# Four-layer gated cross-attention model: the last feed-forward stage is cut into two staggered halves

## Reference

```python
x_norm = x * rsqrt(mean(x*x) + eps)            # x here is the layernormed input
H_res_logits = (x_norm @ W_res.T) + H_res_base # 4 x 4 a token
H_pre_logits, H_post_logits = ...              # 4 each
H_res = sinkhorn_log(H_res_logits)             # 50 iterations, tau 0.1
H_pre, H_post = softmax(H_pre_logits), softmax(H_post_logits)
g = sigmoid(gate)
H_res = (1 - g) * I + g * H_res
x_pre = einsum('btnc,btn->btc', x_streams, H_pre)
y = x_pre @ W_branch
x_mixed = einsum('btij,btjc->btic', H_res, x_streams)
out = x_mixed + einsum('btc,btn->btnc', y, H_post)
x = x + tanh(g_ffn[3]) * out
```

## Time and profile before

| | us |
|---|---|
| median of 3 executions | 1494.13 (1493.41 to 1495.05) |
| the profiled execution, its own time | 1496.6 |
| its span in the trace | 1494.5 |
| TensorE's mean granted clock, share of full speed | 0.954 |

### The profile page before, as it was taken

How to read it: one execution, slowest core, us unless ns; L and a number is a source line. 1 busy time by engine, 2 the same in 40 slices (tenths; PEclk the granted TensorE clock), 3 DMA queues, 4 the chain that set the end, 5 groups by cost and what they waited for, 6 DMA issues and landing times.

```text
span 1494.5 us, 18659 instructions
## 1 busy us (share of the span) xinstructions
PE 1345.3 (90%) x6492; PEld 966.4 (65%) x6492; DVE 1115.3 (75%) x2045; ACT 676.3 (45%) x1405; POOL 336.9 (23%) x386
## 2 busy tenths in 40 slices
PE   7999999999998999968999998999999999999104
PEld 5665566566576558747888865777777777777102
DVE  4788898898888997986555575656666666577998
ACT  4777777787523443432222224443434434343104
POOL 1112112111264020243111031221312221212620
PEclk9999999999999999999999998999999999999557
DMA  5677988798810011243211210101101201000001
GB/s 220 169 180 178 238 219 187 170 244 205 210 69 1 1 57 35 50 94 79 72 56 51 102 43 6 66 29 43 71 29 43 71 29 43 0 1 1 0 0 57
DMA packets 37910, 127.74 MB, mean 85 GB/s; under 512 B 4944, under 2 KB 10960, under 8 KB 31680
## 3 DMA queue, kind: packets, MB, share of 16 engines
q1 hardware_dynamic: 26304, 83.38, 15.9%
q0 software_dynamic: 11520, 43.26, 15.3%
HBM read 72.63 MB, written 10.75 MB: 56 GB/s over the span
## 4 chain that ended last, share of the span: by engine, by line
PE 56%; DVE 23%; DVEq 6%; ACT 5%; DMA 5%; issue 4%; POOL 1%; POOLq 0%; SPq 0%
PE PS L150 12%; PE PS L152 11%; PE PS L151 11%; DVE AR L676 4%; PE PS L925 4%; PE PS L963 4%; DMA AR<-AR 2%; ACT s_sb L606 2%; DVE AR L2654 2%; PE PS L949 2%; DMA nf_in<-in_nf 2%; DVE AR L2643 2%; DVE AR L2650 2%; DVEq L666 1%; DVE AR L682 1%
## 5 line engine op out<-in xcount | busy, mean ns | idle before, releaser
L438 POOL DMA_DIRECT2D AR<-AR x76 | 73.6, 1084 | 330.5 <-DVE AR L695 126.2
L151 PE MATMUL PS<-R16r 128*128 128x512 f32 (+1 forms) x328 | 122.7, 374 | 0.0
L152 PE MATMUL PS<-R16r 128*128 128x512 f32 (+1 forms) x312 | 119.1, 382 | 0.0
L510 PE MATMUL PS<-R,HT 128*128 128x256 f32 x512 | 116.5, 381 | 2.8 <-ACT R L595 2.8
L535 PE MATMUL PS<-R,PT 128*128 128x512 f32 x256 | 116.1, 596 | 2.7 <-DVE X L716 2.7
L510 PEld LDWEIGHTS PS<-R,HT 128*128 128x128 f32 x512 | 94.8, 190 | 15.9 <-ACT R L595 4.3
L1083 ACT COPY AR<-PS 128x512 f32<-128x512 f32 x64 | 37.5, 586 | 146.1 <-PE PS L152 145.7
L606 ACT ACTIVATE s_sb<-PS,sm 128x64 f32<-128x64 f32 x256 | 78.2, 338 | 52.7 <-DVE sm L701 52.1
L150 PE MATMUL PS<-HTr,R16r 128*128 128x512 f32 (+1 forms) x240 | 91.2, 380 | 4.8 <-DVE R16r L190 3.3
L150 PE MATMUL PS<-R16r,HTr 128*128 128x512 f32 (+1 forms) x224 | 90.2, 403 | 0.0
L152 PE MATMUL PS<-HTr,R16r 128*128 128x512 f32 (+1 forms) x240 | 88.2, 368 | 0.0
(11 more groups left out here) (313 smaller groups left out, 3503.1 us busy)
## 6 DMA issues: line engine op xcount, KB each, us to landing
AR<-AR POOLq DMA_DIRECT2D x76, 528.0 KB, 6.2
OR<-in_wo SPq DMA_DIRECT2D x12, 1024.0 KB, 12.7
dequantised<-AR SPq DMA_DIRECT2D x8, 1056.0 KB, 5.8
WR<-in_w0q SPq DMA_DIRECT2D x8, 1024.0 KB, 11.6
AR<-in_w3q SPq DMA_DIRECT2D x8, 1024.0 KB, 4.9
WR<-dequantised SPq DMA_DIRECT2D x22, 256.0 KB, 2.7
AR<-in_nf SPq DMA_DIRECT2D x4, 1056.0 KB, 9.3
nf_in<-in_nf SPq DMA_DIRECT2D x4, 1056.0 KB, 13.3
```

The source lines that it names most:

```text
L151: nc.tensor.matmul(out, ah, bl, start=False, stop=False)
L152: return nc.tensor.matmul(out, al, bh, start=False, stop=last_)
L438: nc.gpsimd.dma_start(nf_below(g)[:, part], what[:, part], accum_op=ALU.add, max_dma_last_dim=4 * N_NF // 2).then_inc(added, 16)
L510: i = nc.tensor.matmul(bank(2 + u % 2)[:, tt * 256:(tt + 1) * 256], HT0[:, c, tok], m[:, :, c * B + b, :], start=c == 0, stop=c == C - 1)
```

## The change

The last stage's chain is made of two halves, tiles 0 to 3 (half 0) and 4 to 7 (half 1), each with logits, small arrays and PSUM bank of its own (KP and KT in banks 6 and 5, logits in banks 7 and 4). The two share VectorE and ScalarE by a written order.

- TensorE: in unit 30 only tiles 0 and 1 are turned ahead of the outputs; tiles 2 and 3 and the logits of tiles 0 to 3 (with the sums of W24) stand behind them, ahead of unit 31's `turn_p`. Tiles 4 and 5 are turned in unit 31.
- ScalarE: table load and gate Exp in unit 29, then half 0's first Exp and Ln at the attention's end. In `act_f3` half 0's column Exp stands between the copies of tiles 6 and 7.
- VectorE: the gate's constants at the end of unit 29; in unit 30 `probs_low` ahead of `shift(31)`; half 0's logits and row maxima in unit 31 where tiles 2 to 5 were normalised. In `dve_f3` half 0's columns, half 1's whole first part and 13 steps of half 0's balancing alternate. Then steps of the two halves by turns; at each half's renewal the other does twelve steps alone. Half 0's mixing matrices come 13 steps of half 1 before half 1's.
- GpSimd: waits for the weights of both halves, then forms x_pre of each half and adds y as before, and at the end mixes tile 3 alone (four multiplications and four additions on 512 columns).
- The tail: TensorE and ScalarE mix tiles 0, 1, 6, 7, VectorE 4 and 2 together and then 5, GpSimd 3. VectorE forms no products. Stores: 0, 3, 1, 6, 2, 4, 7, 5.
- Unchanged: the balancing's steps and their number, 24 and 25 rounds of six for each half, on the same shapes.

The diff, cut to its core:

```diff
@@ pe_x3
                     pe_turn7(pe, 0)
                     pe_turn7(pe, 1)
-                    pe_turn7(pe, 2)
-                    pe_logits(pe, 0)
-                    pe_logits(pe, 1)
                 if u == NU0 - 1:
-                    pe.wait_ge(A3["s_read"], NU0)
-                    pe_turn7(pe, 3)
                     pe_turn7(pe, 4)
-                    pe_logits(pe, 2)
                     pe_turn7(pe, 5)
...
+                if u == NU0 - 2:
+                    pe_turn7(pe, 2)
+                    pe.wait_ge(A3["s_read"], NU0)
+                    pe_turn7(pe, 3)
+                    pe_logits(pe, 0)
@@ act_x3
+                if u == NU0 - 3:
+                    nc.scalar.preload_act_table_set("natural_log_exp_and_others")
+                    nc.scalar.activation(SG[:, 0:1], gate[:], ACT.Exp, scale=-1.0).then_inc(F3["gate_exp"], 1)
+                if u == NU0 - 2:
+                    act_norm(act, 7, (2, 3))
+            act_norm(act, 7, (4, 5))
+            act_rows(act, 0)
+            act_weights(act, 0)
+            act_logarithm(act, 0, 3)
@@ dve_x3
+                if u == NU0 - 2:
+                    probs_low(u)
                 if u + 1 < NU0:
                     shift(u + 1)
-                probs_low(u)
+                if u != NU0 - 2:
+                    probs_low(u)
+                if u == NU0 - 2:
+                    scaled7(dve, (0, 1))
+                if u == NU0 - 1:
+                    f3.logits(0)
+                    f3.rows(0)
...
+                    f3.row_sums(0)
...
+                if u == NU0 - 3:
+                    f3.constants()
@@ pool_f3
+            pool.wait_ge(F3["post"], 2)
+            ahead(0)
+            ahead(1)
+            behind(0)
+            behind(1)
+            pool.wait_ge(F3["mixed"], 1)
+            mix(3, NS)
@@ act_f3
+            act_norm(act, 7, (6,))
+            act_columns(act, 0)
+            act_norm(act, 7, (7,))
+            act_logarithm(act, 0, 5)
+            act_kernels(act, 0, 6)
+            act_rows(act, 1)
...
+            branch(0)
+            branch(1)
+            act_factors(act, 0)
+            act_kernels(act, 0, 8)
+            act_factors(act, 1)
+            act_kernels(act, 1, 8)
+            weighted(0)
+            weighted(1)
+            mixed_tile(0)
+            weighted(2)
+            mixed_tile(1)
+            weighted(3)
+            mixed_tile(2)
+            mixed_tile(3)
@@ VectorF3
+            def after_last(self, h):
+                if self.last[h]:
+                    self.dve.wait_ge(F3["scaled_half"], self.last[h])
...
+        def dve_f3(dve, f3):
+            f3.columns(0)
+            scaled7(dve, (2,))
+            f3.column_sums(0)
+            scaled7(dve, (3,))
+            f3.shifted_columns(0)
+            scaled7(dve, (4,))
+            f3.logits(1)
+            f3.rows(1)
+            f3.kernels_ready(0, 7)
+            f3.balance(0, 3)
+            f3.row_sums(1)
+            f3.balance(0, 3)
+            f3.columns(1)
+            scaled7(dve, (5, 6, 7))
+            f3.column_sums(1)
+            f3.balance(0, 3)
+            f3.shifted_columns(1)
+            f3.balance(0, 4)
+            f3.kernels_ready(1, 7)
+
+            def turns(h):
+                while f3.left(0) and f3.left(1):
+                    f3.balance(0, 1)
+                    f3.balance(1, 1)
+                assert f3.left(h) == 0
+
+            def renew(h):
+                f3.factors(h)
+                f3.balance(1 - h, 6)
+                f3.refresh(h)
+                f3.balance(1 - h, 6)
+                f3.kernels_ready(h, 10)
+            turns(0)
+            renew(0)
+            turns(1)
+            renew(1)
+            turns(0)
+            f3.mixing(0)
+            f3.balance(1, f3.left(1))
+            f3.mixing(1)
+            dve.wait_ge(F3["posted"], 2)
+            for group in ((4, 2), (5,)):
@@ block.sync
-            for t in (4, 5, 0, 1, 6, 7, 2, 3):
+            for t in (0, 3, 1, 6, 2, 4, 7, 5):
```

More of the change, by code:

```diff
@@ new lines, in ahead @@
+            def ahead(h):
+                pool.wait_ge(F3["post"], h + 1)
+                for n in range(NS):
+                    dst = XTMP if n else XP[h]
+                    nc.gpsimd.tensor_tensor(dst.rearrange("p (t c) -> p t c", t=TH), rows7(h)[:, :, n, :],
+                                            tiles(PP[h])[:, :, n].unsqueeze(2).to_broadcast([P, TH, P]), ALU.mult)
+                    pool.drain()
+                    if n:
+                        nc.gpsimd.tensor_tensor(XP[h], XP[h], XTMP, ALU.add)
+                        pool.drain()
+                pool.drain().then_inc(F3["pre"], 1)
+                nc.gpsimd.tensor_tensor(PP[h], PP[h], tg[:, 1, 3:4].to_broadcast([P, TH * 2 * NS]), ALU.mult)
+                pool.drain()
@@ new lines, in behind, with mix @@
+            def behind(h):
+                pool.wait_ge(F3["y_sb"], h + 1)
+                for k in range(TH):
+                    add_spread(TH * h + k, Y[h][:, k * P:(k + 1) * P], tiles(PP[h])[:, k, NS:2 * NS], NS)
+                pool.drain().then_inc(F3["posted"], 1)
+            def mix(t, parts):
+                for j in range(NS):
+                    add_spread(t, hn_of(7, t)[:, j * P:(j + 1) * P], tiles(K3[0])[:, t, j:parts * NS:NS], parts)
+                pool.drain().then_inc(F3["done_pool"], 1)
@@ new lines, in act_columns, with act_kernels, act_factors, branch @@
+        def act_columns(act, h):
+            act_asked(act, h, 4)
+            act_run(K3[h], Z[h], ACT.Exp)
+        def act_kernels(act, h, n):
+            act_asked(act, h, n)
+            act_run(KP[h], Z[h], ACT.Exp)
+            act_run(KT[h].rearrange("p (t j i) -> p t j i", t=TH, j=NS), matrices(Z[h]).rearrange("p t i j -> p t j i"),
+                    ACT.Exp)
+        def act_factors(act, h):
+            act_asked(act, h, 7)
+            act_run(RC[h], RC[h], ACT.Ln)
+        def act_f3(act):
+            def branch(h):
+                act.wait_ge(F3["preT_mm"], h + 1)
+                nc.scalar.copy(XPT[h], bank(3)).then_inc(F3["preT"], 1)
+                act.wait_ge(F3["y_mm"], h + 1)
+                nc.scalar.copy(Y[h], bank(3)).then_inc(F3["y_sb"], 1)
+            def weighted(k):
+                t = PE_TILES[k]
+                h = t // TH
+                act.wait_ge(F3["mixed"], h + 1)
+                for j in range(NS):
+                    for i_ in range(NS):
+                        i = nc.scalar.activation(products(k, j)[:, i_ * P:(i_ + 1) * P],
+                                                 hn_of(7, t)[:, j * P:(j + 1) * P], ACT.Copy,
+                                                 scale=tiles(K3[h])[:, t % TH, i_ * NS + j:i_ * NS + j + 1])
+                    i.then_inc(F3["prod_act"], 1)
```

511 lines of the change are left out of this document (244 added, 267 removed).

## The result

The changed kernel takes 1502.65 us (median of 5 runs, 1501.35 to 1503.9); the kernel before, run beside it, 1494.24 us (5 runs, 1493.41 to 1495.05). The ratio is 1.0053, 95% interval 1.004 to 1.0066: slower by 8.4 us (6.0 to 9.9). The forecast was 1497.3, +3.2, and its range ended at 1501.5. The direction was right; the size was too small by more than half. The profiled execution has a span of 1499.9 us and its own time is 1501.63.

The account below looks back on a forecast made before the run. VectorE's own instruction order was taken to set every time from 1370.8 us to the end. The terms +1.5 + 1.8 - 2.7 + 3.0 - 0.4 = +3.2 on 1494.1 gave 1497.3 us, range 1491.5 to 1501.5.

Parts of the forecast that it names:

- Part C: Balancing of both halves, from H to M0: forecast -2.7 us, 80.5 against 83.2 before.
- H: Instant of the balancing's first multiplication, half 1's in the changed kernel: 1386.8 us before, forecast 1390.1.
- M0: Instant when half 0's mixing matrices are ready and the tail begins: forecast 1470.6 us.
- Part A: Order in the attention's last units, up to P: forecast +1.5 us, bounds +0.2 and +2.2.
- P: Instant when the subtraction behind the last unit's turned probabilities ends: 1371.4 us before, forecast 1372.9.
- The rival that TensorE keeps its clock in unit 30: Attention's last units: Part A costs only 0.2 us, total +1.9, 1496.0 us; chance 0.15.
- Part B: From P to H, with half 1's first balancing work: forecast +1.8 us, 17.2 against 15.4 before.
- Part D: Tail from M0 to VectorE's last addition: forecast +3.0 us, M0 + 23.6 against 20.6 before.
- the rival without a lock: Tail: VectorE's additions pass between GpSimd's operations, ScalarE ends at M0 + 21.5; total +1.5, 1495.6 us; chance 0.18.
- the rival of TensorE as the bound: Tail: TensorE stays at its lower clock, twenty matmuls take 36 us, end 13 later, 1510 us; chance 0.05.
- Stores: Behind the last result: only tile 5's store, 3.5 us instead of two in 3.9, -0.4; bounds 3.2 and 3.9.
- lone steps are cheap: Balancing where one half runs alone: 0.13 us a step, 4.8 less in all, total -1.6, 1492.5 us; chance 0.10.

Follow-up runs that it names:

- Leads 12 and 14: Changed kernel with half 0 leading by 12 or 14 balancing steps instead of 13: 1500.39 us (ratio to before 1.0029) and 1501.79 us (one run).
- split order: Changed kernel with the sums and logits of tiles 0 and 1 ahead of unit 30's outputs, those of tiles 2 and 3 behind: 1499.74 us, ratio 1.0024.
- PSUM version of the other tail: Kernel before, GpSimd mixing tile 4, ScalarE and TensorE 5 to 7, VectorE 0 to 3 with partial sums in PSUM: 1491.82 us, ratio 0.9974.
- SBUF version: Kernel before, GpSimd mixing tile 4, ScalarE and TensorE 5 to 7, VectorE 0 to 3 with partial sums in SBUF: 1499.85 us, ratio 1.0032.
- lead 12 and split logits: Changed kernel with half 0 leading by 12 steps and the logits of tiles 0 and 1 moved ahead of unit 30's outputs: 1497.02 us, ratio 1.0018.

## Why the prediction was wrong, by its steps

**Part C is the term that failed: -2.7 forecast, +0.3 measured.** The prediction took "131 pairs 35.1" and "137 pairs 36.7" at the 0.268 of the kernel before. The 13 steps of lead put the halves at different kinds of step, and a pair took 0.278: 269 pairs of 0.0105 more are 2.8 us. The other 0.3 is in the two renewals, (83.55 - 269 x 0.2783 - 0.96)/2 = 3.9 against 3.7; the prediction had put six lone steps at 1.5 there, where its own 0.268 makes 1.6. Only part C had the gain that was to pay for the rest. The error was to carry over the cost of a pair as a property of the instructions, when it had been measured in one phase alone. Leads 12 and 14 show it: with equal kinds side by side H to M0 takes 81.7 and 81.0, near the 80.5 forecast. What makes unequal kinds slower stays open.

**Part A, +1.5 forecast, +2.4 measured.** The mechanism (TensorE between the outputs and the turn is what P waits for, at a low clock) was right, its place was not. "I take the same 4.3" for the outputs: they ran at full clock in 2.9 (1360.36 to 1363.26). "0.85 a group: 4.2" for sums and logits: they took 0.8 and 5.0, as the clock fell in the logits instead. The two errors nearly cancel (-1.4 and +1.6), so that part A came as near as it did is partly luck. The turn came at 1369.95, 1.1 sooner than the forecast's 1371.0 in an execution that was 1.5 ahead; counted from the scores, 13.72 against 13.3. From the turn to P it took 2.35 and not 1.9, because the turn, too, ran at half clock (1.09 for its four transposes against 0.76). The rival that TensorE keeps its clock in unit 30 was right of the outputs and wrong of P. Only the split order kept the clock up to P, with 13.49, near the rival's 13.67 + 0.2.

**Part B, +1.8 forecast, +2.6 measured.** The nine half-size steps of logits and maxima took 2.44 and 2.40 and not 2.1 each: 0.6 of the 0.8. On eight tiles nine steps are about 2.8, an estimate from 2.40 for the eight of L2584 to L2603 and 0.43 for one more as wide as L2584 (1380.72 to 1381.15 in the kernel before). So half the elements save 0.05 a step; the prediction had 0.07, and 0.3 for the step in front. The rest was right: the additions and last statistics 3.6 (3.6), columns and normalised tiles of half 0 2.8 (2.75), 13 lone steps 3.1 (3.0), half 1's sums and shift 2.2 with the turn at L2720, 0.60 beside GpSimd's first operations (2.15 with the 0.4 foreseen).

**Part D, +3.0 forecast, +3.0 measured** (VectorE M0 + 23.55 against 23.6; ScalarE M0 + 21.56 against 21.5). VectorE and GpSimd take turns on two SBUF inputs, as the earlier trace rows had shown, and the rival without a lock is out. So is the form in which VectorE gets nothing through until GpSimd is done (M0 + 24.0): between 1477.79 and 1484.45 VectorE got seven instructions through beside five of GpSimd's, the last five of them beside three. The Trainium skill ("SBUF — State Buffer", Who interferes with whom) says that whoever issues first keeps the shared ports for its whole instruction and the other is blocked. The trace agrees, instruction by instruction (1.28 beside 1.27, 1.07 beside 1.05); the prediction had stretched that rule over all of GpSimd's work. That the sum comes out to 0.1 is partly luck: half 1's matrices were themselves held up and came 1.75 later than forecast (the additions start at M0 + 6.45 and not M0 + 4.7), but GpSimd was done 0.8 sooner (M0 + 10.6 against 11.4) and the additions behind it took 13.0 against 12.2, 0.48 of it a gap between the two groups. TensorE's clock was 0.86 from M0 to the end, and it bound nothing: the rival of TensorE as the bound is out.

**Stores, -0.4 forecast, -1.5 measured:** one 256 KB store behind the last result took 2.46 here (2.43 to 2.49 in six traces of this tail), below the lower bound of 3.2. I had shortened a figure for two stores too little. It isn't a constant: one store took 2.49 in the PSUM version of the other tail and 3.45 in its SBUF version, and why is open.

**Lone steps cost 0.267** (1474.23 to 1475.03 for three), as forecast, and "lone steps are cheap" is out. The Trainium skill ("VectorE: DVE Perf Modes", The DRAIN you can't avoid) says that eight copies take the same time with a semaphore after each as with one after the last. That doesn't carry over to steps that each wait for the one before: here 0.267 a step alone against 0.134 an instruction with two chains.

**Range and chances.** The sum was +3.2; with -2.7 replaced by +0.3, 1.5 by 2.4, 1.8 by 2.6 and -0.4 by -1.5 it is the ledger's +6.9 within rounding. For part C the bounds had cheaper lone steps and 1 us for GpSimd's tail, and nothing for the price of a pair, though this was the largest gain. What stays open is the remaining 1.5 us between the two traces and the medians, which the interval of the ratio covers.

## What to carry to other kernels

A per-instruction cost read in one alternation holds for that alternation: when two dependent chains are interleaved with another offset, check which kinds of step stand side by side, and choose the offset. When matmuls are moved, ask where the clock falls next, and break up rows of narrow matmuls rather than shift them. Before GpSimd is given work beside VectorE, move one of VectorE's two SBUF inputs to PSUM; and see first which engine and which store end last, since removing the turns alone gained 0.6 us here.

## What the runs showed of the hardware that was not expected

- Two interleaved chains of small VectorE instructions take 0.268 us a pair when two of a kind follow one another and 0.278 when no two do; a chain alone takes 0.267 a step, so a second chain beside it is free in the first case.
- One order of the balancing gives one time: H to M0 is 83.55, 83.54 and 83.59 in three kernels with lead 13, and 83.22 and 83.21 in two traces of before, while what lies ahead of the stage scatters by 3.2.
- L2778, a TENSOR_SCALAR on 16 elements that reads one SBUF tensor, was held up beside GpSimd too (1.07 for 0.24, and 1.22 with lead 12 and split logits), while sums and reciprocals beside GpSimd kept their 0.22 and 0.25. The Trainium skill ("SBUF — State Buffer", Who interferes with whom) counts tensor_scalar among the operations that can enter a mode that takes the ports shared with GpSimd, when their operands meet its conditions; no run here shows that mode.
- One store of 256 KB behind the last result took 2.43 to 2.49 us in seven traces and 3.45 in an eighth; two behind one another took 3.84 to 4.42.
